# A transformer layer on one core: K, Q, V and sums moved in fewer, larger DMAs, and the last stage's loads split by what waits for them

## The reference

```python
x = x + attn(_layernorm(x))        # logits = (q k) * 4, softmax over keys, @ v, @ Wo.T + bo
x = x + ffn(_layernorm(x))
# ffn: x_prev = x shifted by one token
#      xr = mu_r*x + (1-mu_r)*x_prev ;  xk = mu_k*x + (1-mu_k)*x_prev
#      sigmoid(xr @ W_r.T) * (square(relu(xk @ W_k.T)) @ W_v.T)
```

## Time and profile before

| | us |
|---|---|
| median of three runs | 3090.06 |
| lowest and highest | 3086.84, 3092.26 |
| the profiled execution's own time | 3085.56 |
| its span, first to last instruction | 3083.8 |

### The profile page before, as it was taken

How to read it: one execution, slowest core, us unless ns; L and a number is a source line. 1 busy time by engine, 2 the same in 40 slices (tenths; PEclk the granted TensorE clock), 3 DMA queues, 4 the chain that set the end, 5 groups by cost and what they waited for, 6 DMA issues and landing times. The chain is left out here.

```text
span 3083.8 us, 68918 instructions
## 1 busy us (share of the span) xinstructions
PE 2840.5 (92%) x25812; PEld 1041.6 (34%) x25812; DVE 2571.1 (83%) x5088; ACT 2513.4 (82%) x2767; POOL 324.5 (11%) x497
## 2 busy tenths in 40 slices
PE   8999999999999999999999999999999999978887
PEld 5452232323222222222222323222323222226665
DVE  7669898989898989899898989898989898925443
ACT  5568898989898989889898989898989898965443
POOL 6660000000000000000000000000000000014332
PEclk9999999999999999999999999999999999999999
DMA  5651000000000000000000000000000000023331
GB/s 167 191 151 39 20 20 20 21 20 20 20 20 20 21 20 19 20 16 21 17 20 20 20 20 21 20 20 20 21 20 20 20 21 15 26 60 118 102 110 62
DMA packets 155279, 124.97 MB, mean 41 GB/s; under 512 B 63696, under 2 KB 139344, under 8 KB 154960
## 3 DMA queue, kind: packets, MB, share of 16 engines
q1 hardware_dynamic: 154960, 120.57, 13.9%
HBM read 72.75 MB, written 47.19 MB: 39 GB/s over the span
## 5 line engine op out<-in xcount | busy, mean ns | idle before, releaser
L619 ACT ACTIVATE a_p<-psum 128x1024 f32<-128x1024 f32 x2048 | 1989.2, 1023 | 264.1 <-PE psum L842 153.5
L701 DVE TENSOR_REDUCE a_mx<-psum 128x1 f32<-128x512 f32 x3092 | 1971.5, 686 | 215.0 <-PE psum L889 198.8
L918 PE MATMUL psum<-a_p,a_vst 128*32 128x256 f32 (+1 forms) x15872 | 1257.9, 401 | 5.7 <-ACT a_p L619 0.9
L889 PE MATMUL psum<-a_ks,a_qs 48*128 48x512 f16 x3594 | 708.0, 385 | 134.5 <-issue 47.0
L842 PE MATMUL psum<-a_qs,a_ks 50*128 50x512 f16 x4096 | 806.4, 386 | 13.6 <-ACT a_p L619 9.7
L918 PEld LDWEIGHTS psum<-a_p,a_vst 128*32 128x32 f32 x15872 | 342.8, 108 | 626.1 <-issue 521.1
L889 PEld LDWEIGHTS psum<-a_ks,a_qs 48*128 48x128 f16 x3594 | 212.9, 93 | 645.2 <-issue 535.9
L842 PEld LDWEIGHTS psum<-a_qs,a_ks 50*128 50x128 f16 x4096 | 203.4, 93 | 523.2 <-ACT a_p L619 294.8
L696 DVE CUSTOM_DVE_ANT_0 a_copied<-psum,a_copied 128x512 f32<-128x512 f32 x502 | 326.8, 689 | 47.4 <-PE psum L889 33.5
L564 POOL COPY a_vst<-a_vin 128x64 f32<-128x64 f32 x256 | 59.7, 236 | 2320.0 <-PE psum L918 2320.0
L628 ACT ACTIVATE a_copied<-psum 128x1024 f32<-128x1024 f32 x251 | 258.9, 1031 | 13.5 <-PE psum L855 13.4
(11 more groups left out here) (101 smaller groups left out, 1269.1 us busy)
## 6 DMA issues: line engine op xcount, KB each, us to landing
a_ks<-k_parts SPq DMA_DIRECT2D x192, 64.0 KB, 2.1
a_qs<-q_parts SPq DMA_DIRECT2D x384, 32.0 KB, 1.8
p_x<-x SPq DMA_DIRECT2D x16, 512.0 KB, 4.2
v_rows<-p_v SPq DMA_DIRECT2D x64, 128.0 KB, 2.4
q_parts<-p_parts SPq DMA_DIRECT2D x32, 256.0 KB, 2.7
k_parts<-p_parts SPq DMA_DIRECT2D x32, 256.0 KB, 3.2
a_vin<-v_rows SPq DMA_DIRECT2D x64, 128.0 KB, 2.4
numerators<-a_o SPq DMA_DIRECT2D x256, 32.0 KB
```

Of the source, the lines that this page charges most:

```text
L619: ac.activation(p_sb[:, c % 2, 2 * half:2 * half + 2, :], psum[:, at:at + 2, :], ACT.Exp, scale=SCALE).then_inc(s_exp, 1)
L701: dve.tensor_reduce(mx[:, q, kb:kb + 1], psum[:, bank(at), :], AX.X, ALU.max).then_inc(s_mx, 1)
L889: te.matmul(psum[:, bank(slot(n, par)), :], qs[row:row + SR, pit % QRING, at:at + P], keys, start=True, stop=True).then_inc(s_sp, 1)
L918: mm = te.matmul(psum[32 * g:32 * g + 32, O, at:at + width], v_st[:, c, g, :], p_sb[:, c % 2, g, at:at + width], start=(c == 0), stop=(c = ...
```

## The change

Its parts, with the numbers of DMAs:

1. Stores of a projected block: V in one DMA instead of 4 (`v_rows` is now laid out by sequence, so that one piece of V is read in runs of 64 numbers instead of 256), Q, K and KD in one each instead of 2, issued in the order Q, V, K, KD.
2. K of one piece in 2 DMAs instead of 3, one of them copying the first part twice by a leading dimension of step 0; KD the same, on a semaphore of its own (`s_kd`), which only `differences` waits for.
3. The first pieces are spread over blocks 4 to 12: K of the first pair in blocks 4 and 5, K of the second in 7 and 8, V and KD later.
4. `out`: numerators and denominators of a head in one DMA of 17 rows, 4 DMAs instead of 8.
5. Mix: numerators by 2 DMAs and inverse denominators by 2 instead of 16 (a middle dimension of step 0), on a semaphore of their own; x by one DMA instead of 2, also on its own. They are issued as soon as their buffers are free, up to 7 blocks ahead.
6. GpSimd in the mix: `heads` and `add_to_x` apart, and the order in pairs: finish(n-1), heads and add of n+4, of n+5, finish(n).

```diff
-OUTPUTS = 2 * G
-STORES = 4 + 4 + 2
+OUTPUTS = G
+STORES = 4
+LOADS = 2
...
+    def rows_of_k(self, sp, dst, src, sem):
+        high = len(PAIRS) - 1
+        sp.dma_start(dst[0:high * D], src[0].unsqueeze(0).to_broadcast([high, D, src.shape[-1]])).then_inc(sem, DMA)
+        sp.dma_start(dst[high * D:SR], src[1]).then_inc(sem, DMA)
...
+    def first(self, sp, blk):
+        n = blk - QB
+        if n in (0, 1):
+            self.first_k(sp, n)
+        if n in (3, 4):
+            self.first_k(sp, n - 1)
+        if n in (0, 5, 6):
+            self.first_q(sp, max(n - 4, 0))
+        if n in (2, 4):
+            self.first_v(sp, n - 2)
+            self.first_v(sp, n - 1)
+        if n in (7, 8):
+            self.first_kd(sp, 2 * (n - 7))
+            self.first_kd(sp, 2 * (n - 7) + 1)
...
+    def load_heads(self, sp, blk):
+        s, seq, tok = blk % 2, blk // BPB, bass.ds((blk % BPB) * TB, TB)
+        if blk >= 2:
+            self.gf.wait(sp, blk - 2, "h1")
+        for k in range(KH):
+            heads = slice(k * self.HH, (k + 1) * self.HH)
+            sp.dma_start(self.num[s][:, k, :], self.sums_d[seq, heads, 0:D, tok]).then_inc(self.s_head[s], DMA)
+            sp.dma_start(self.rden[s][:, k, :], self.rden_d[seq, heads, tok].unsqueeze(1).to_broadcast(
+                [self.HH, D, TB])).then_inc(self.s_head[s], DMA)
+    def load_x(self, sp, blk):
+        if blk >= 2:
+            self.dx.wait(sp, blk - 2, "x11")
+        sp.dma_start(self.x_sb[blk % 2][:, :, :], self.x_v[blk, :, :, :]).then_inc(self.s_x[blk % 2], DMA)
...
                 for g in range(G):
-                    head, row = grp * G + g, 32 * g
-                    sp.dma_start(num_d[bass.ds(head * D, D), bass.ds(seq * N + qb * TB, TB)],
-                                 o_sb[row:row + D, :]).then_inc(s_out, DMA)
-                    sp.dma_start(den_d[seq, bass.ds(head, 1), bass.ds(qb * TB, TB)],
-                                 o_sb[row + D:row + D + 1, :]).then_inc(s_out, DMA)
+                    sp.dma_start(sums_d[seq, grp * G + g, :, bass.ds(qb * TB, TB)],
+                                 o_sb[32 * g:32 * g + D + 1, :]).then_inc(s_out, DMA)
...
                     inputs.load_k(sp, it + G)
+                    inputs.load_kd(sp, it + G)
                     inputs.load_v(sp, it + G)
...
-            for blk in range(2, 6):
-                inputs.load(sp, blk)
-            inputs.store_inverse(sp, B - 1)
-            sp.wait_ge(inputs.s_rden[B - 1], DMA)
-            for blk in range(BLOCKS):
+            for blk in range(2, 4):
+                inputs.load_heads(sp, blk)
+            for blk in range(2, 4):
+                inputs.load_x(sp, blk)
+            for blk in range(4, 6):
+                inputs.load_heads(sp, blk)
+            for blk in range(0, BLOCKS, 2):
+                if blk:
+                    back(blk - 1)
+                for n in range(2):
+                    if blk + 4 + n < BLOCKS:
+                        inputs.load_x(sp, blk + 4 + n)
+                    if blk + 6 + n < BLOCKS:
+                        inputs.load_heads(sp, blk + 6 + n)
+                if blk == 0:
+                    inputs.store_inverse(sp, B - 1)
+                    sp.wait_ge(inputs.s_rden[B - 1], DMA)
                 back(blk)
-                if 6 <= blk + 5 < BLOCKS:
-                    inputs.load(sp, blk + 5)
...
-            for blk in range(BLOCKS):
+                inputs.add_to_x(pool, blk)
+            for blk in range(0, BLOCKS, 2):
+                if blk:
+                    finish(blk - 1)
                 if blk + 4 < BLOCKS:
-                    inputs.heads(pool, blk + 4)
+                    for n in range(4, 6):
+                        inputs.heads(pool, blk + n)
+                        inputs.add_to_x(pool, blk + n)
                 finish(blk)
+            finish(BLOCKS - 1)
```

More of the change, by code:

```diff
@@ L107, in __init__ @@
         self.s_k = ctx.enter_context(nc.semaphore("a_s_k"))
+        self.s_kd = ctx.enter_context(nc.semaphore("a_s_kd"))
         self.s_q = ctx.enter_context(nc.semaphore("a_s_q"))
@@ L117, in set_unit, with place_of, load_kd @@
         pool.wait_ge(self.s_unit, 2 * buf + par + 1)
-    def load_k(self, sp, piece):
[L121 to L129, removed]
+    def rows_of_k(self, sp, dst, src, sem):
+        high = len(PAIRS) - 1
+        sp.dma_start(dst[0:high * D], src[0].unsqueeze(0).to_broadcast([high, D, src.shape[-1]])).then_inc(sem, DMA)
+        sp.dma_start(dst[high * D:SR], src[1]).then_inc(sem, DMA)
+    def place_of(self, piece):
+        g = piece % G
+        return (piece // H, (piece // (H // KH)) % KH, bass.ds((piece % (H // KH)) * D, D), (piece // G) % 2,
+                bass.ds((g % 2) * HALF, SR), g // 2)
+    def load_k(self, sp, piece):
+        seq, kh, channels, buf, rows, pair = self.place_of(piece)
+        self.rows_of_k(sp, self.ks[rows, buf, pair, :], self.k_d[seq, kh, :, channels, :], self.s_k)
+    def load_kd(self, sp, piece):
+        seq, kh, channels, buf, rows, pair = self.place_of(piece)
+        self.rows_of_k(sp, self.kd[rows, buf, pair, :], self.kd_d[seq, kh, :, channels, TB:2 * TB], self.s_kd)
     def load_q(self, sp, it):
@@ L142, in load_v, with first_k @@
     def load_v(self, sp, piece):
[L143 to L147, removed]
+        c, unit = (piece % G) * (CH // G), piece // G
+        sp.dma_start(self.v_in[:, unit % 2, bass.ds(c, CH // G), :],
+                     self.v_d[unit // G, :, bass.ds(c, CH // G), bass.ds((unit % G) * G * D, G * D)]
+                     ).then_inc(self.s_v, DMA)
+    def first_k(self, sp, n):
         if n == 0:
@@ L199, in __init__ @@
         self.s_den, self.s_rden = ([sem(f"m_s_{n}{seq}") for seq in range(B)] for n in ("den", "rden"))
-        self.s_in = [sem(f"m_s_in{s}") for s in range(2)]
+        self.s_head, self.s_x = ([sem(f"m_s_{n}{s}") for s in range(2)] for n in ("head", "x"))
         self.s_num = sem("a_s_out")
@@ L252, in heads, with add_to_x @@
                                             self.rden[s][:, k, :], ALU.mult))
+    def add_to_x(self, pool, blk):
+        s = blk % 2
+        pool.wait_ge(self.s_x[s], DMA * (blk // 2 + 1))
         if blk == 0:
@@ L274, in add_bias, with stage_attend @@
         dve.tensor_tensor(self.bo_sb[:, :], self.bo_sb[:, :], bank, ALU.add).then_inc(self.s_bias, 1)
-def stage_attend(nc, psum, x, wqT, wkT, wvT, bq, bk, q_d, k_d, kd_d, v_d, num_d, den_d, inputs, ahead):
+def stage_attend(nc, psum, x, wqT, wkT, wvT, bq, bk, q_d, k_d, kd_d, v_d, sums_d, inputs, ahead):
     LEAD = 5
@@ L360, in stage_attend @@
         s_one = sem("a_s_one")
-        s_k, s_q, s_v = inputs.s_k, inputs.s_q, inputs.s_v
+        s_k, s_kd, s_q, s_v = inputs.s_k, inputs.s_kd, inputs.s_q, inputs.s_v
         s_vc = sem("a_s_vc")
@@ L452, in store @@
                 s, seq, tb = blk % 2, blk // BPB, blk % BPB
[L453 to L464, removed]
+                least.wait(sp, blk, f"part1_q{KH - 1}")
+                sp.dma_start(q_d[blk].rearrange("h a p t -> p (h a) t"), parts[s][:, 0:KH, :, :].rearrange(
+                    "p h a t -> p (h a) t")).then_inc(s_wr[s], DMA)
+                av.wait(sp, blk, "v1")
+                sp.dma_start(v_d[seq, :, bass.ds(tb * TT, TT), :], v_sb[s][:, :, :]).then_inc(s_wr[s], DMA)
+                least.wait(sp, blk, f"part1_k{KH - 1}")
+                sp.dma_start(k_d[seq, :, :, :, bass.ds(tb * TB, TB)].rearrange("h a p t -> p (h a) t"),
+                             parts[s][:, KH:2 * KH, :, :].rearrange("p h a t -> p (h a) t")).then_inc(s_wr[s], DMA)
+                least.wait(sp, blk, f"part1_kd{KH - 1}")
+                sp.dma_start(kd_d[seq, :, :, :, bass.ds(tb * (TB // 2), TB // 2)].rearrange("h a p t -> p (h a) t"),
+                             kd_parts[s][:, :, :, :].rearrange("p h a t -> p (h a) t")).then_inc(s_wr[s], DMA)
             def rows(it):
@@ L520, in _ @@
                         stored(sp, QB - 2 + s)
-                if QB <= blk < QB + G:
-                    inputs.first(sp, blk - QB)
+                if blk >= QB:
+                    inputs.first(sp, blk)
                 store(blk)
@@ L526, in _ @@
             sp.wait_ge(inputs.s_unit, 4)
+            for sem in (s_k, s_kd):
+                sp.wait_ge(sem, K_INC * G)
+            sp.wait_ge(s_v, V_INC * G)
+            sp.wait_ge(s_q, Q_INC * (QRING - 1))
             for it in range(ITS):
@@ L536, in _ @@
                         sp.wait_ge(ahead.s_rden[0], DMA)
-                        ahead.load(sp, n)
+                        ahead.load_heads(sp, n)
+                        ahead.load_x(sp, n)
                 body(it)
@@ L587, in _ @@
                 ahead.heads(pool, n)
+                ahead.add_to_x(pool, n)
         @block.scalar
@@ L851, in differences @@
                 at = pair * TB + t * P
+                te.wait_ge(s_kd, K_INC * (pit // QB * G + 2 * (pair + 1)))
                 after(te, s_exp, u - 1)
@@ L1366, in build @@
```

(5 more changed lines are left out.)

52 lines of the change are left out of this document (23 added, 29 removed).

## The result

| | before | changed |
|---|---|---|
| median, us (4 runs each) | 3088.45 | 3115.19 |
| lowest to highest | 3084.44 to 3092.26 | 3113.88 to 3118.89 |
| span of the profiled execution | 3083.8 | 3117.1 |

The ratio is 1.0089 (95% interval 1.0071 to 1.0106): slower by 27 us. The prediction was 3097 with a range of 3066 to 3130: the direction and the range held, and the time came 18 us above the value.

What follows compares the result with a forecast made beforehand. PE, busy 92% of the span, was taken as the bound. Terms −9.65 + 51 − 4 − 28.1 − 2.6 = +6.65 us on the median 3090.06 gave 3096.7, said as 3097, range 3066 to 3130.

Steps and rivals of the forecast that it cites:

- Changes of units: In attention, PE waits longer for K behind the sums on one DMA engine: +51 us, bounds +39 to +64.
- The slope of 0.043: At changes of units, the assumed landing time in us per KB on one DMA engine, between 0.039 and 0.047.
- First pieces: In projection block 6, earlier K loads remove PE's wait and the slow clock after it: −9.65 us, bounds −9.65 to 0.
- Start of the last stage: PE's first proj after attention comes sooner, with fewer loads delaying it: −4 us, bounds −8 to +1.
- Pairs of the last stage: From proj(3) to proj(15), six block pairs at 33.8 us each, loads off the path: −28.1 us, bounds −45 to −3.
- 4 + 1 issues: In the last stage, fewer load issues, up to 7 blocks ahead, take the loads off the path.
- Tail: At proj(15), the slow clock goes with the wait before it: −2.6 us, bounds −2.6 to 0.
- Rival A: At changes of units, 17 rows and K's copy spread over 16 engines, stalls vanish: −72 for +51, 2974 us; chance 0.12.
- Rival B: At changes of units, sums on one engine but K's copy spread: +14 and not +51, 3060 us; chance 0.08.
- rival C: The last stage keeps about 38 us a pair, GpSimd competing with DVE for memory: 3122 us; chance 0.18.

Runs made afterwards that it cites:

- sums_split: The changed kernel with each head's sums stored as 16 rows and 1 row again (8 DMAs), K still in 2 DMAs; 3076.53 us, ratio 0.9965.
- keys_kd_earlier: The changed kernel with K and KD of the fourth piece loaded one iteration earlier, transfer shapes kept; 2977.70 us, ratio 0.9645.
- whole_kd_earlier: As keys_kd_earlier, with the sums of an iteration in one DMA of all 128 rows; 2973.96 us, ratio 0.9636.
- heads_lead: As whole_kd_earlier, with block 2's heads loaded ahead of the last out, block 3's and x before the wait for last sums; 2974.23 us, ratio 0.9626.
- rows_again: The changed kernel with 16 one-row DMAs of inverse denominators a block again (19 loads and not 5); 3121.50 us, ratio 1.0113.
- keys_split: The changed kernel with K of one piece in 3 DMAs again, sums still 17 rows in one DMA; 3083.79 us, ratio 0.9981.
- sums_alone: The kernel before with only each head's sums merged into one DMA of 17 rows; 3121.49 us, ratio 1.0114.

## Why the prediction came out as it did

- **Changes of units: the mechanism right, the term undersized.** Forecast +51, measured +65.7, just above the bound of +64. PE stopped at +4.15 as said. The stall was 6.96 us for 6.3, and the slow clock behind it 2.5 us for 2.2 (9.5 less 6.96); over the first 6 us after the wait the granted clock was 0.53. The packets confirm one engine for 17 rows and two for the copy. The slope of 0.043 was right for K (0.041 and 0.042). In the changed kernel the shortfall lies in the four DMAs of sums: 136 KB took 8.17 us where 1.7 + 0.043 × 136 gives 7.5; at 0.047, the steeper of the prediction's two slopes, it is 8.1. That is not all of it: in sums_split, with the sums spread again, the stall is above its figure too, by 0.7 us, which stays open.
- **First pieces:** −9.65 forecast, −10.5 measured. But the working named "issued in blocks 4 and 5, ahead of what follows them"; the order is worth 1 us, and the earlier issue came mostly without it. The number fits in part for another reason than the one given.
- **Start of the last stage:** −4 forecast; measured −5.6 at proj(0) and +7.6 up to proj(3), together +2, outside the bounds of −8 to +1. The reason named was right, DVE's and GpSimd's first works falling together, but it cost more than the 4.3 us allowed: DVE was busy 7.0 us longer with the same 47 instructions. In five kernels (before, changed, keys_kd_earlier, whole_kd_earlier, heads_lead) the stretch from proj(0) to proj(3) is 31.45, 39.02, 37.83, 34.06 and 34.67 us and DVE's busy time in it 17.95, 24.93, 24.17, 19.81 and 20.59, so the difference stays between 13.5 and 14.3. The cause is read from what overlaps in the traces; no run kept the two engines apart.
- **Pairs of the last stage:** 33.8 forecast, 33.81 measured from proj(7) to proj(13), and the limiter that comes next (DVE's m_x, 2.65 us) was named. Over proj(3) to proj(15) −26.6 for −28.1. The reason given was half wrong: "4 + 1 issues" plays no part (rows_again); the lead is what is left.
- **Tail:** −2.6 forecast, −0.8 measured. Proj(15) is fast now (3.69), but the slow clock comes at the last value product instead (5.41 us for 3.72).

Rival A would have been right about issue alone, and it fell by the packets' count. Its time is nearly what keys_kd_earlier reaches (2977.70 for 2974), because it priced what the stalls are worth. Rival B fell with keys_split, where spreading K's copy took 2.3 us off the stall, and rival C with the pairs of 33.81.

The terms other than the changes of units sum to −32.4 in the spans (−10.5, +2, −26.6, −0.8, and +3.5 in the rest of attention, which had no term), against −44 forecast; the changes of units to +65.7 against +51. That is 26.7 us above the forecast sum of +6.65 in the spans. The medians show only 18 of it: the profiled execution of before lies 4.5 us under the median that the prediction started from, and that of the changed kernel 3.7 us above its own. This 8 us is chance, and it made the predicted time look better than its sum. The direction hung on +51 against −44 and was given a chance of 0.50.

## What to carry to other kernels

Before merging DMAs, look at the outermost dimension of the result: here 16 rows and 1 row went over 16 engines and one, 17 rows went over one, and a copy of two made by a leading step of 0 went over two. Count the small packets of the profile, they tell which it was. Then ask what waits behind such a transfer: moving the loads that wait by one iteration took some 137 us off, where splitting both transfers took some 89 (by the ratios, 0.9645 and 0.9800 against 1.0089).

## What the runs showed of the hardware

Joining a row to 16 others cost more than it saved in issue (35 us in sums_alone), though the DMA engines together were busy under a tenth of the time through attention (the page's row DMA is 0 there). On one engine the sums, in rows of 2 KB, took 0.047 us per KB ((8.17 − 3.33) / 102) and K, in rows of 4 KB, 0.042, one DMA behind the other. The loss behind a stall grows little with its length: 2.0 us behind 3.1 (76.7 / 15 less 3.13), 2.5 behind 7.0. It was gone where the stall was gone, in keys_kd_earlier. And two DVE instructions (L1310) took 3.5 us where GpSimd worked beside them and 1.40 where it did not.
